# Two pairs of banks for the column scores and one for the row scores in the last attention of a four-layer network

## What is computed

```python
xn = (x - mu) / jnp.sqrt(var + EPS) * ln_gamma + ln_beta
qkv = jnp.einsum('bsh,oh->bso', xn, W_qkv) + b_qkv
scores = jnp.einsum('bhqd,bhkd->bhqk', q, k) / jnp.sqrt(jnp.asarray(HD, x.dtype))
probs = jax.nn.softmax(scores, axis=-1)
ctx = jnp.einsum('bhqk,bhkd->bhqd', probs, v)
out = jnp.einsum('bsh,oh->bso', ctx, W_out) + b_out
return x + out
```

## Time and profile before

| what | value |
|---|---|
| median of 3 runs | 1702.48 us (1701.78 to 1707.01) |
| profiled execution | 1700.83 us, its span 1699.1 us |
| span outside of the last attention's products | 0 to 1311.42 us and from about 1571.8 us |
| row maxima, first start to last end | 1312.07 to about 1528.31 us |
| last column scores with no row scores beside them | 1528.61 to 1551.84 us (end of the last exponential) |
| busy in 1300 to 1580 us: row maxima on DVE, exponentials on ACT | 151.9 us, 139.1 us |
| TensorE's granted clock, mean over the span | 0.857 of 2.4 GHz |

### The profile page before, as it was taken

How to read it: one execution, slowest core, us unless ns; L and a number is a source line. 1 busy time by engine, 2 the same in 40 slices (tenths; PEclk the granted TensorE clock), 3 DMA queues, 4 the chain that set the end, 5 groups by cost and what they waited for, 6 DMA issues and landing times. The chain is left out here.

```text
span 1699.1 us, 23331 instructions
## 1 busy us (share of the span) xinstructions
PE 1241.2 (73%) x8169; PEld 704.7 (41%) x8177; DVE 855.5 (50%) x2251; ACT 611.6 (36%) x1233; POOL 499.1 (29%) x547
## 2 busy tenths in 40 slices
PE   2745999996577858999977874842922888887294
PEld 2532555554464535556544632431621122222163
DVE  5034555652025557677635487860045778892102
ACT  1211444443223124666442132310411367664141
POOL 5333012102240056666100021244433111102442
PEclk9975999998797978999998987765965599999597
DMA  9422421201631027655409000021422111200233
GB/s 228 118 67 68 95 67 32 71 11 26 193 93 33 1 66 207 175 169 165 117 1 134 15 7 0 1 66 47 129 73 65 57 52 43 70 23 12 84 118 106
DMA packets 148284, 131.84 MB, mean 78 GB/s; under 512 B 19215, under 2 KB 131779, under 8 KB 148176
## 3 DMA queue, kind: packets, MB, share of 16 engines
q1 hardware_dynamic: 128480, 108.81, 24.0%
q10 hardware_dynamic: 13040, 9.77, 2.3%
q0 software_dynamic: 6656, 11.88, 2.1%
HBM read 82.91 MB, written 48.40 MB: 77 GB/s over the span
## 5 line engine op out<-in xcount | busy, mean ns | idle before, releaser
L1984 DVE TENSOR_REDUCE att_maxima<-psum 128x2 f32<-128x1024 f32 (+3 forms) x384 | 356.0, 952 | 199.0 <-PE psum L1641 99.8
L1855 ACT ACTIVATE att_probs<-psum 128x512 f32<-128x512 f32 (+1 forms) x640 | 322.1, 553 | 277.9 <-PE psum L1674 127.9
L101 POOL TENSOR_TENSOR rstd<-var_eps,neg_half 128x4 f32<-128x4 f32 x52 | 53.4, 1026 | 634.6 <-DVE var_eps L92 634.6
L1690 PE MATMUL psum<-att_probs,att_values 128*32 128x512 f32 (+3 forms) x1536 | 167.0, 510 | 2.7 <-ACT att_context_t L1862 2.5
L733 POOL DMA_INDIRECT returned<-moe_out,moe_slot_tokens x112 | 107.9, 963 | 186.3 <-DVE moe_out L695 161.8
L136 PE MATMUL psum<-ident,normalised_rows 128*128 128x128 f32 x192 | 44.0, 373 | 139.5 <-DVE normalised_rows L110 138.1
L1657 PE MATMUL psum<-att_queries,att_keys 50*128 50x512 bf16 (+3 forms) x512 | 121.5, 357 | 23.1 <-ACT att_probs L1855 15.8
L1622 PE MATMUL psum<-att_keys,att_queries 48*128 48x512 bf16 (+3 forms) x512 | 94.3, 383 | 44.4 <-DMA att_keys<-score_terms 27.5
L632 ACT ACTIVATE moe_hidden<-psum,moe_b 128x320 f32<-128x320 f32 (+1 forms) x128 | 77.6, 607 | 135.4 <-PE psum L580 134.8
L587 PE MATMUL psum<-moe_w,moe_hidden 128*128 128x128 f32 (+1 forms) x896 | 110.5, 279 | 12.9 <-ACT moe_hidden L632 12.9
L587 PEld LDWEIGHTS psum<-moe_w,moe_hidden 128*128 128x128 f32 (+1 forms) x896 | 101.9, 184 | 22.5 <-ACT moe_hidden L632 12.8
(11 more groups left out here) (245 smaller groups left out, 2124.1 us busy)
## 6 DMA issues: line engine op xcount, KB each, us to landing
score_terms<-att_parts SPq DMA_DIRECT2D x44, 384.0 KB, 2.6
moe_w<-l_w SPq DMA_DIRECT2D x64, 256.0 KB, 3.0
moe_back<-returned SPq DMA_DIRECT2D x24, 256.0 KB, 4.1
att_queries<-score_terms SPq DMA_DIRECT2D x64, 96.0 KB
att_keys<-score_terms SPq DMA_DIRECT2D x64, 96.0 KB
att_queries<-score_terms SPq DMA_DIRECT2D x16, 384.0 KB, 4.3
att_keys<-score_terms SPq DMA_DIRECT2D x16, 384.0 KB, 5.8
dispatched<-untaken SPq DMA_DIRECT2D x2, 2064.0 KB, 28.9
```

Source lines behind the costliest of these rows:

```text
L1690: mm = nc.tensor.matmul(o_bank[VW * j:VW * (j + 1), first_query[s]:T], values[:, b % 2, s, GH * (G % GROUPS) + j, :], probs[:, G % 2, j, o ...
L1855: nc.scalar.activation(probs[:, G % 2, 2 * p + r, unit_at[u]:unit_at[u] + w], g.psum[:, cols_bank + r, 0:w], ACT.Exp).then_inc(probs_ready, 1)
L1984: ins = nc.vector.tensor_reduce(maxima[:, G % 2, t, 2 * p:2 * p + 2], g.psum[:, rows_bank(k):rows_bank(k) + 2, c0:c0 + w], axis=AX, op=ALU ...
```

## The change

In the attention without a causal mask the row scores now have one pair of banks (0 and 1) and the column scores two (2, 3 and 4, 5 in turn). `rows_unit` of unit k waits until DVE has finished unit k - 1, and `columns_unit` of unit k until ACT has read unit k - 2. In each unit the column matmuls now stand ahead of the row matmuls. In the two causal attentions the constants and the order come out as before.

```diff
-        rows_bank = lambda k: 2 * (k % 2)
-        cols_bank = 4
+        ROW_RING, COL_RING = (2, 1) if causal else (1, 2)
+        rows_bank = lambda k: 2 * (k % ROW_RING)
+        cols_bank = lambda k: 2 * ROW_RING + 2 * (k % COL_RING)
...
             def rows_unit(G, p, u):
                 i, k = G % RING, G * X + p * U + u
-                if k >= 2:
-                    pe.wait_ge(rows_taken, k - 1)
+                if k >= ROW_RING:
+                    pe.wait_ge(rows_taken, k - ROW_RING + 1)
...
             def columns_unit(G, p, u, r):
-                i, k, j = G % RING, 2 * (G * X + p * U + u) + r, 2 * p + r
-                if k >= 2:
-                    pe.wait_ge(probs_ready, k - 1)
+                i, k, j = G % RING, G * X + p * U + u, 2 * p + r
+                if k >= COL_RING:
+                    pe.wait_ge(probs_ready, 2 * (k - COL_RING) + r + 1)
...
                     p, u = divmod(x, U)
-                    if R:
+                    if R and causal:
                         rows_unit(n + 2, p, u)
                     if C:
                         if x == 0:
                             pe.wait_ge(max_loaded[n % 2], 16 * max_loads * (n // 2 + 1))
                         for r in range(2):
                             columns_unit(n, p, u, r)
+                    if R and not causal:
+                        rows_unit(n + 2, p, u)
...
-                                         g.psum[:, cols_bank + r, 0:w], ACT.Exp).then_inc(probs_ready, 1)
+                                         g.psum[:, cols_bank(G * X + x) + r, 0:w], ACT.Exp).then_inc(probs_ready, 1)
```

More of the change, by code:

```diff
@@ L1647, in columns_unit @@
             def columns_unit(G, p, u, r):
-                i, k, j = G % RING, 2 * (G * X + p * U + u) + r, 2 * p + r
-                if k >= 2:
-                    pe.wait_ge(probs_ready, k - 1)
+                i, k, j = G % RING, G * X + p * U + u, 2 * p + r
+                if k >= COL_RING:
+                    pe.wait_ge(probs_ready, 2 * (k - COL_RING) + r + 1)
                 c0 = 0
                 for s in units[u]:
-                    dst = g.psum[:, cols_bank + r, c0:c0 + width[s]]
+                    dst = g.psum[:, cols_bank(k) + r, c0:c0 + width[s]]
                     key, query = slice(s * P, (s + 1) * P), slice(first_query[s], T)
@@ L1673, in columns_bias @@
                         for n in range(PARTS):
-                            mm = nc.tensor.matmul(g.psum[:, cols_bank + r, c0:c0 + w], g.flipb[:], bias_kq[:, h, n, 0:w],
+                            mm = nc.tensor.matmul(g.psum[:, cols_bank(0) + r, c0:c0 + w], g.flipb[:], bias_kq[:, h, n, 0:w],
                                                   start=False, stop=n == PARTS - 1, skip_group_check=True)
                     else:
-                        mm = nc.tensor.matmul(g.psum[:, cols_bank + r, c0:c0 + P], g.identb[:], g.mask_kq[:],
+                        mm = nc.tensor.matmul(g.psum[:, cols_bank(0) + r, c0:c0 + P], g.identb[:], g.mask_kq[:],
                                               start=False, stop=True, skip_group_check=True)
```

## The result

| what | before | after |
|---|---|---|
| median, runs side by side | 1702.16 us (1701.78 to 1707.01, 4 runs) | 1739.09 us (1734.93 to 1744.18, 4 runs) |
| ratio to before | | 1.0202, 95% interval 1.0162 to 1.0242 |
| profiled execution, span | 1700.83 us, 1699.1 us | 1734.93 us, 1733.2 us |
| slots -2 to 1 | 50.30 us | 65.69 us |
| slots 2 to 13 | 165.97 us | 189.14 us |

A forecast was written before the change was run, and what follows sets the result against it. The prediction took one row pair to make DVE's reductions and PE's row scores a chain setting the pace. Losses of 17.1 and 15.3 us less 2.9 gained gave 29.5 us, so 1732 us, own range 1725 to 1740.

The forecast's parts named there:

- slots -2 to 1: First part of the last attention, priced at the low clock: 67.4 us for 50.3, a loss of 17.1 us.
- slots 2 to 13: Middle part of the last attention, 96 rounds of 1.70 us plus extra work: 181.3 us for 165.97, 15.3 lost.
- terms: Parts summed for a stretch: rounds, plus DVE or PE work exceeding them; in slots 2 to 13, 181.3 us.
- The chain: Last attention: reduction, row scores, next reduction in sequence with one row pair; 1.70 us per unit, 1.93 at low clock.
- The soft spot: DVE's reduction after a wait takes 1.23 us, or perhaps 1.16, which would be 9 us less, 1723 us.
- price of the low clock: A pair of units after the change takes 4.82 us at the low clock for 3.40, 1.42 us more.
- the clock's rival: PE's clock stays low or falls: 1749 us if it rises three slots late, 1800 if never; chance 0.14.
- the argument against it: In slots 14 and 15 a pair took 2.88 us, with less PE work per stretch, and the clock held.
- Slots 14 and 15: End of the last attention, no row scores left: the second column pair closes gaps before exponentials, 2.9 us gained.
- The signs: Last attention: reductions idle about 0.47 us, row weight loads wait over 90 us, column ones nearly nothing, stretch 249 us.
- The column side as the bound: Rival: the second column pair frees PE, slots 2 to 13 run at DVE's pace, 1670 us; chance 0.02.
- The loss of half: Rival: `take_values` and normalised rows don't add, slot 1 isn't slower, half the shorter reductions; +15 us, 1717 us; chance 0.06.

The follow-up runs named there:

- half reduction: The changed kernel, but each reduction of the last attention reads 256 of the 512 keys; 1695.95 us, ratio 0.9933 to the kernel before.
- banks only: The changed kernel's banks, but row matmuls ahead of column matmuls as in the kernel before; 1745.63 us, ratio 1.0228 to before.
- one pair each: The changed kernel, but column scores also have one pair of banks, two banks unused; 1759.06 us, ratio 1.0292 to the kernel before.
- columns twice: The changed kernel, but each column matmul of the last attention is issued twice; 1745.34 us, ratio 1.0233 to the kernel before.
- 3 / 3: The changed kernel, but three banks each for row and column scores, handed out singly, with reductions by head; 1703.60 us, ratio 0.9989 to the kernel before.
- order only: The kernel before with its banks, but column matmuls ahead of row matmuls; 1705.33 us, ratio 1.0015 to before.
- contexts in halves: The kernel before, but each context step is cut into two halves of 256 queries, spread over the units; 1694.61 us, ratio 0.9927 to before.

## Why the prediction held

The time, 1739.09 us, lies in the forecast's own range of 1725 to 1740, by 0.9 us. Two stretches came out close to their terms and one didn't, and that it stayed in the range is in part luck: slots 2 to 13 lost 7.8 us more than summed, and the other two stretches gave 3.2 us of that back.

**The chain** of 1.70 and 1.93 us measured 1.71 and 1.94. The half reduction shows that it is a chain. The soft spot, a reduction of 1.16 or 1.23 us behind a wait, measured 1.22 or 1.23, with a mean of 1219 ns.

**Slots -2 to 1**, +17.1 predicted, +15.4 measured. The miss is slot 1. Its four contexts were priced at the low clock throughout (8 x 1.93 + 3.8 = 19.2 us), but the clock rose at about 1373 and the slot took 16.5. Slots -2 to 0 were 49.2 us for some 48.1.

**Slots 2 to 13**, +15.3 predicted, +23.2 measured. This is the step that was mis-sized. The terms, put together by slot, beside the distances of the casts:

| slot | 2 | 3 | 4 | 5 | 6 | 7 | 8 | 9 | 10 | 11 | 12 | 13 |
|---|---|---|---|---|---|---|---|---|---|---|---|---|
| terms | 14.8 | 14.8 | 16.4 | 14.3 | 16.7 | 14.8 | 16.4 | 14.3 | 17.0 | 13.9 | 13.9 | 14.3 |
| measured | 14.7 | 16.1 | 16.7 | 14.3 | 18.4 | 17.2 | 16.7 | 15.7 | 17.4 | 13.9 | 13.9 | 14.3 |

The seven slots without a fall are within 0.3 us. The five with one (3, 6, 7, 9 and 10) make up 7.2 of the 7.8 us. By the prediction's own price of the low clock, 1.42 us in a pair of 4.82, the 26.5 us at that level cost 26.5 / 4.82 x 1.42 = 7.8 us. This fits only in the sum: slot 10 lies just 0.4 us over its terms with 7 us at the low clock, slot 7 2.4 us. The two other kernels with one pair of row banks and no added work bear both the terms and the price out. In banks only slots 6 and 10 had no fall and took 16.5 and 16.9 us, for terms of 16.7 and 17.0. Over slots 2 to 13 the terms and the price make 181.3 + 16.4 = 197.7 us for banks only (measured 199.2) and 181.3 + 17.6 = 198.9 us for one pair each (199.7). So the forecast's mechanism and the clock's rival both happened, and the sum left the second out. By the prediction's own sign, falls in several slots, it is the clock as well, though the rival's 1749 us did not come. What was wrong is the argument against it, that the clock had held in slots 14 and 15 with less work: this told nothing of slots 3 to 10. No run has the falls alone taken away, since columns twice removed most of them but added work. Why PE's clock falls is open.

The Trainium skill, page "TensorE: Matmul & The Clock Gate", section "A second HAM failure mode: psum-queue depth-cycling", says that the clock can swing as PE idles between PSUM banks. This trace agrees in direction (26.5 us low for 6.6, in five places), but the kernels with 3 / 3 fell too. The same page, section "HAM oscillation — how this bites in real kernels", reports of another kernel that PSUM double-buffering gave no further gain. That doesn't hold for the row banks here (+2.3% for banks only); it does for the column banks in slots 11 to 13.

**Slots 14 and 15**, -2.9 predicted, -4.4 measured. One pair each against banks only or after gives 3.8 for the second pair. The other 0.6 us also shows in order only (22.87 for 23.50). ACT waited only 1.5 us for column scores in these slots of after.

**The signs.** Reductions idle 0.49 us (0.47 announced), 70.7 us in all (over 60). Row weight loads wait 124.6 us for DVE (over 90). Column weight loads wait 23.7 us for ACT, where nearly nothing was announced: 16.3 us of it lie in slots 2 to 13, where the slots without a fall still met terms that hold no such wait, and 6.5 us in the last two slots, where ACT sets the pace. The whole stretch was 254.8 us for 249.

**The rivals.** The column side as the bound is refuted by the result, slower where it had faster, and by one pair each, where the second pair gave nothing in slots 11 to 13. The loss of half (15 us) is refuted by the 37 us measured, and by slots 11 to 13, which come out at their full terms.

## What to carry to other kernels

Before a buffer is moved from one user to another, write down the round that remains with one buffer: release, refill, consumer. If it is longer than the pace of the unit, the loss is that difference for each unit, whatever the other side gains; here 1.71 us against a pace of about 1.55, and the other side gained only where no row scores were left. A round with waits in it may also bring clock falls, which belong in the sum with a price and not only among the rivals. Cutting the long step behind which the short ones stand (contexts in halves) gave 0.7%, which the banks didn't.

## What was not expected of the hardware

- How often the clock fell differed more than PE's waits would suggest. Low time in slots 2 to 13 was 6.6 us before, 26.5 after, 55.8 and 59.9 in the other two kernels with one pair of row banks, but also 30.7 and 34.0 in the two with 3 / 3, where PE was busy for 149.73 of 170.39 us, and 7.6 in columns twice. Each is one profiled execution, and no run settles what decides it.
- In slots -2 to 1 of before PE stayed at 1.2 GHz for some 48 us (1312 to about 1360) before the clock rose, with PE busy for 18.30 of 20 us on the way and for 9.49 of the last 10. In the other runs the rise came elsewhere, in after 59 us behind the first reduction. A window of before:

```profile
1330.00:1350.00 20.00, 18.30 (x61) 4.69 (x60) 16.02 (x20) 11.54 (x21) 3.54 (x4) 0.50 0.35 111
```

- The blocks ahead of the last attention varied by up to 16 us between profiled executions (first reduction at 1312.07 to 1327.70 us) though no kernel changed them, so stretches were compared by their own length.
